# Split-precision mixture-of-experts kernel on one Trainium2 core: first loads and first gate products in another order, down products five steps behind, and f16 parts in one adapter

## What is computed

```python
g = einsum('bsd,edf->ebsf', x, Wg);  u = einsum('bsd,edf->ebsf', x, Wu)
expert_outs = einsum('ebsf,efd->ebsd', silu(g) * u, Wd)
expert_output = einsum('be,ebsd->bsd', gating_probs, expert_outs)
shared = (silu(x @ Sg) * (x @ Su)) @ Sd
x = x + (1 - sg) * expert_output + sg * shared
h = relu(einsum('bsh,bha->bsa', x, W1[lang]) + b1[lang])        # 128 -> 32
y = x + einsum('bsa,bah->bsh', h, W2[lang]) + b2[lang]          # 32 -> 128
x = x + (y - mean(y)) * rsqrt(var(y) + 1e-5) * gamma[lang] + beta[lang]
```

## Time and profile before

| | |
|---|---|
| median of 3 runs | 297.24 us |
| lowest, highest | 296.75, 297.40 us |
| profiled execution, its time | 297.04 us |
| its span, first to last instruction | 295.2 us |
| granted TensorE clock | 0.999 of full speed |
| instructions in the span | 5086 |
| ScalarE busy | 231.1 us, 517 instructions |
| GpSimd busy | 19.3 us, 32 instructions |

### The profile page before, as it was taken

The page is one execution under the profiler, slowest core; times in us unless marked ns, Lnnn a source line. Parts: engine busy times, 40 slices in busy tenths (PEclk is TensorE's granted clock), DMA queues, the critical chain, the costliest instruction groups (busy, mean ns, idle before and its releaser), DMA issues.

```text
span 295.2 us, 5086 instructions
## 1 busy us (share of the span) xinstructions
PE 290.1 (98%) x1510; PEld 144.3 (49%) x1510; DVE 268.8 (91%) x585; ACT 231.1 (78%) x517; POOL 19.3 (7%) x32
## 2 busy tenths in 40 slices
PE   8999999999999999999999999999999999999995
PEld 2444444444444444444444444444444444588883
DVE  5999999998989898988989999999999999977795
ACT  6998878788878787877897788887878876667771
POOL 3200201100000000000002010001100011000011
PEclk9999999999999999999999999999999999999999
DMA  6973110244000000000011001010001110000001
GB/s 208 385 307 109 52 65 19 62 120 112 2 2 0 0 2 0 0 2 1 1 22 26 18 9 39 12 25 19 17 3 39 27 18 10 2 36 3 0 2 36
DMA packets 17940, 13.39 MB, mean 45 GB/s; under 512 B 11486, under 2 KB 15994, under 8 KB 17914
## 3 DMA queue, kind: packets, MB, share of 16 engines
q1 hardware_dynamic: 17482, 12.86, 14.4%
q10 hardware_dynamic: 432, 0.21, 0.2%
HBM read 11.23 MB, written 1.05 MB: 42 GB/s over the span
## 4 chain that ended last, share of the span: by engine, by line
PE 94%; DVE 2%; DMA 1%; SPq 1%; issue 1%; ACT 0%; POOL 0%; POOLq 0%; DVEq 0%
PE moe_ps L449 10%; PE moe_ps L446 10%; PE moe_ps L447 10%; PE gate_ps L400 10%; PE up_ps L426 10%; PE up_ps L431 10%; PE up_ps L423 10%; PE gate_ps L403 10%; PE gate_ps L408 10%; DMA w_full<-weights 1%; DVE hidden L680 1%; PE adapt_ps L458 0%; DVE gx_lo L649 0%; SPq L319 0%; DVE h_lo L686 0%
## 5 line engine op out<-in xcount | busy, mean ns | idle before, releaser
L563 ACT ACTIVATE silu<-gate_ps 128x512 f32<-128x512 f32 (+1 forms) x160 | 88.2, 551 | 45.3 <-PE gate_ps L408 44.3
L680 DVE SCALAR_TENSOR_TENSOR hidden<-silu,up_ps 128x512 f32<-128x512 f32 (+1 forms) x160 | 100.3, 627 | 19.2 <-PE up_ps L431 11.6
L686 DVE TENSOR_TENSOR h_lo<-hidden,h_hi 128x512 f16<-128x512 f32 (+1 forms) x160 | 102.4, 640 | 0.2
L568 ACT ACTIVATE h_hi<-hidden 128x512 f16<-128x512 f32 (+1 forms) x160 | 92.8, 580 | 9.2 <-DVE hidden L680 8.4
L426 PE MATMUL up_ps<-gx_lo,w_hi 128*128 128x512 f16 (+1 forms) x160 | 57.3, 358 | 0.4 <-DVE gx_lo L649 0.4
L400 PE MATMUL gate_ps<-x_hi,w_hi 128*128 128x512 f16 (+1 forms) x160 | 57.4, 359 | 0.0
L431 PE MATMUL up_ps<-gx_hi,w_lo 128*128 128x512 f16 (+1 forms) x160 | 57.3, 358 | 0.0
L423 PE MATMUL up_ps<-gx_hi,w_hi 128*128 128x512 f16 (+1 forms) x160 | 57.3, 358 | 0.0
L403 PE MATMUL gate_ps<-x_lo,w_hi 128*128 128x512 f16 (+1 forms) x160 | 57.3, 358 | 0.0
L446 PE MATMUL moe_ps<-h_hi,w_hi 128*128 128x512 f16 (+1 forms) x160 | 57.3, 358 | 0.0
L449 PE MATMUL moe_ps<-h_lo,w_hi 128*128 128x512 f16 (+1 forms) x160 | 57.3, 358 | 0.0
(11 more groups left out here) (88 smaller groups left out, 148.6 us busy)
## 6 DMA issues: line engine op xcount, KB each, us to landing
w_full<-weights SPq DMA_DIRECT2D x8, 768.0 KB, 9.2
affine_sb<-affine SPq DMA_DIRECT2D x16, 128.0 KB, 2.9
x_full<-xT SPq DMA_DIRECT2D x3, 256.0 KB, 8.6
x<-x_blocks SPq DMA_DIRECT2D x48, 16.0 KB, 1.8
out_dram<-result SPq DMA_DIRECT2D x3, 256.0 KB, 2.1
w_full<-weights SPq DMA_DIRECT2D x4, 128.0 KB, 3.0
w_full<-w2b SPq DMA_DIRECT2D x24, 16.0 KB
w_full<-weights SPq DMA_DIRECT2D x1, 256.0 KB, 3.8
```

The lines of the kernel that those rows point to most:

```text
L563: nc.scalar.activation(silu_slot(n), gate_ps[n % 2][:, 0:STEPS[n][4]], ACT.Silu, scale=1.0 / W_SCALE).then_inc(silu_ready, 1)
L568: nc.scalar.activation(h_slot(h_hi, n), hidden_slot(n), ACT.Copy).then_inc(h_hi_ready, 1)
L680: nc.vector.scalar_tensor_tensor(out=hidden_slot(n), in0=silu_slot(n), scalar=HIDDEN_RESCALE, in1=up_ps[n % 2][:, 0:STEPS[n][4]], op0=ALU. ...
L686: nc.vector.tensor_tensor(h_slot(h_lo, n), hidden_slot(n), h_slot(h_hi, n), ALU.subtract).then_inc(h_lo_ready, 1)
```

## The change

1. **First loads.** SyncE issues both halves of tile 0 first, then weight pieces 1, 2, 3, tile 1, piece 4, and only then the gating probabilities of experts 1 to 7. ScalarE's queue issues piece 0 and then the first gating probabilities.
2. **First gates.** `first_gates` makes gate(0) and gate(1) in halves of 256 columns, six products for the first half of `x` and six for the second.
3. **First splits.** ScalarE does w_hi of piece 1 ahead of the four gx_hi, pieces 2 and 3 after silu of steps 0 and 1, gx_hi of group 1 at steps 1 and 2, and piece 4 at step 3. h_hi and h_lo of step 0 come at step 3, of steps 1 and 2 at step 4, of 3 and 4 at step 5, and from then on one step behind. VectorE does x_lo of the first half ahead of w_lo of piece 0, w_lo of piece 3 at step 0 and of piece 4 at step 3.
4. **Down products.** down(0) to down(7) stand five steps behind, and step 12 has three, down(7), down(8) and down(9). From down(9) on the lag is three as before. `h_hi` and `h_lo` have six slots for four, `hidden` four for three.
5. **Adapter of the last tile's first half.** W1, W2, x2T and h are split into f16 parts, four more operations on ScalarE and four on VectorE: those of W1 at steps 132 and 133, of W2 at 136 and 137, of x2T at 148, of h at 152. TensorE does six products with W1 and four with an f16 identity in place of the two transposes, after step 150, and six with W2, into one bank, after step 154. Relu is at step 151, the copy of x2 at 152, statistics and result each one step later, with one addition for both batches in place of two. W2 lies in `half_w2`. GpSimd sets the row of ones and makes the f16 identity.

The core of the diff:

```diff
+FIRST_LAG = 5
+H_SLOTS = 6
-HIDDEN_SLOTS = 3
+HIDDEN_SLOTS = 4
 def down_at(n):
-    return n + LAG + min(max(n - len(WHOLE) - len(HALVES) // 2, 0), END_LAG - LAG)
+    first = max(FIRST_LAG - LAG - max(n - 2 * CHUNKS + 1, 0), 0)
+    return n + LAG + first + min(max(n - len(WHOLE) - len(HALVES) // 2, 0), END_LAG - LAG)
...
 def in_at(j):
-    return 1 if j < MOVED else 2
+    return 1 if j < MOVED else 3
 def back_at(j):
-    return 6
+    return 6 if j < MOVED else 7
...
+HIDDEN_PARTS_AT = {n + 1: [n] for n in range(5, LAST)}
+HIDDEN_PARTS_AT.update({3: [0], 4: [1, 2], 5: [3, 4]})
...
-            load_first(0)
-            sp.dma_start(cols(x_full, 0, HALF), xT[0, :, 0:HALF]).then_inc(x0_loaded[0], 16)
+            for half in range(2):
+                sp.dma_start(cols(x_full, half, HALF), xT[0, :, half * HALF:(half + 1) * HALF]).then_inc(x0_loaded[half], 16)
             for i in (1, 2, 3):
                 load_first(i)
-                if i == 1:
-                    sp.dma_start(gates_in[:, 2 * B:], gates[:, 2 * B:]).then_inc(gates_loaded, 16)
             sp.dma_start(cols(x_full, 1, N), xT[1]).then_inc(x_loaded[0], 16)
             load_first(4)
+            sp.dma_start(gates_in[:, 2 * B:], gates[:, 2 * B:]).then_inc(gates_loaded, 16)
...
+            def first_gates():
+                pe.wait_ge(w_first_hi_ready, 1)
+                for half in range(2):
+                    x_at = slice(half * HALF, (half + 1) * HALF)
+                    pe.wait_ge(x_hi_ready, half + 1)
+                    for n in range(2):
+                        nc.tensor.matmul(gate_ps[n][:, x_at], expert_w(w_hi, 0, 0, n), x_hi[:, x_at], start=True, stop=False)
...
+            def half_in(j):
+                pe.wait_ge(y_ready, BEFORE[j])
+                pe.wait_ge(half_w1_lo_ready, 1)
+                pe.wait_ge(half_x2T_lo_ready, 1)
+                for of_w, of_x in ((half_w1_hi, half_x2T_hi), (half_w1_lo, half_x2T_hi), (half_w1_hi, half_x2T_lo)):
+                    for q in range(PAIRS):
+                        last = nc.tensor.matmul(fourth(adapt_ps, q)[:, 0:S], cols(of_w, q, A), cols(of_x, q, S),
...
+                for q in range(PAIRS):
+                    nc.tensor.matmul(cols(x2_ps, q, S), cols(half_x2T_hi, q, S), ident_half[:, :], start=True, stop=False)
+                    last = nc.tensor.matmul(cols(x2_ps, q, S), cols(half_x2T_lo, q, S), ident_half[:, :], start=False,
+                                            stop=True)
...
+                    nc.tensor.matmul(psum, h_hi_q, w2_hi_q, start=True, stop=False)
+                    nc.tensor.matmul(psum, h_hi_q, w2_lo_q, start=False, stop=False)
+                    last = nc.tensor.matmul(psum, h_lo_q, w2_hi_q, start=False, stop=True)
...
+            act.dma_start(w_full[:, low:high], weights[0, :, low:high]).then_inc(w0_loaded[0], 16)
+            nc.scalar.preload_act_table(ACT.Silu)
             act.dma_start(gates_in[:, 0:2 * B], gates[:, 0:2 * B]).then_inc(first_gates_loaded, 16)
-            nc.scalar.preload_act_table(ACT.Silu)
-            act.dma_start(cols(x_full, 1, HALF), xT[0, :, HALF:]).then_inc(x0_loaded[1], 16)
```

More of the change, by code:

```diff
@@ L200, in build @@
         x2_ps = bank("x2_ps")
[L201 removed]
+        half_back_ps = moe_ps[(TILES - 1) % 2]
         last_tile = TILES - 1
@@ L460, in adapter_in @@
                 last.then_inc(adapt_done, 1)
-                if j < MOVED:
-                    return
-                pe.wait_ge(consts_ready, 1)
-                for q in range(first, first + count):
-                    last = nc.tensor.transpose(cols(x2_ps, q, S), cols(x2T, q, S), ident[:, :])
-                last.then_inc(x2_transposed, 1)
             def adapter_back(j):
-                _, first, count, _ = JOBS[j]
                 pe.wait_ge(ones_ready, 3)
@@ L478, in adapter_back @@
                     return
-                pe.wait_ge(adapt_h_ready, count)
-                pe.wait_ge(x2_ready, 1)
-                for q in range(first, first + count):
-                    last = nc.tensor.matmul(cols(back_ps[q % 2], q // 2, D), stacked(adapt_h, q, S, A + 1),
-                                            stacked(w2b2_sb, q, D, A + 1), start=True, stop=True)
-                last.then_inc(back_done, 1)
+                half_back()
             pe.wait_ge(warm_ready, 1)
```

194 lines of the change are left out of this document (146 added, 48 removed).

## The result

| | before | changed |
|---|---|---|
| median | 297.62 us (11 runs, 296.75 to 298.54) | 299.3 us (11 runs, 298.77 to 300.54) |
| profiled execution | 297.04 us | 298.9 us |
| its span, granted clock | 295.2 us, 0.999 | 297.0 us, 0.997 |

The changed kernel takes 1.0055 times as long, 95% interval 1.004 to 1.007: slower by 1.64 us. The forecast was slower, 298.3; the time lies above it and just outside the range, which ended at 299.1. 0.38 of the 1.0 us of difference is only the median of before, 297.24 in the three runs shown and 297.62 in these eleven: on the base of 297.24, from which the forecast was added up, the ratio gives 298.9, inside the range. The rest is in the sum, which gave +1.05 where the two spans differ by 1.8.

What follows compares the result with a forecast made beforehand. TensorE was taken as the bound (busy 290.1 of 295.2 us), VectorE close behind. Opening +1.51, adapter -0.46 and end 0 sum to +1.05 on the median 297.24, giving 298.3 us; range 297.1 to 299.1.

Steps and rivals of the forecast that it cites:

- The mechanism: Opening: TensorE reaches step 8 1.29 us of work earlier, stands for VectorE's w_lo of expert 1's up third; chance 0.66.
- the start of gx_hi in the part on the first loads: ScalarE's opening: second weight piece lands at 4.27, w_hi runs from 4.33, gx_hi from about 4.7 instead of 4.31.
- The price of 0.45 for a gx_lo held by GpSimd's x_lo: VectorE's opening: gx_lo at 9.8 held until 10.25 by GpSimd's later x_lo; bounds 0 and 0.9.
- the signs that I had named: Changed trace: step 8 pause, w_lo ending near 20.4, x_lo about 8.9, gx_lo lengthened, L473 of step 4 delayed, adapter 0.55 and 0.33.
- The term: Opening up to step 8: L431 0.22 later with 1.29 still to do, +1.51 us; bounds 0 and +1.9.
- The adapter: Last tile's first half in f16 parts: in -0.16, back -0.19, pause of 0.11 gone; together -0.46, from -0.7 to -0.1.
- the end: Last steps: h_lo(159) ends at about 289.0, where the last product wants it at 289.01; costs 0, at most +0.25.
- the splits of the adapter: Steps 132 to 152: four more operations each on ScalarE and VectorE cost nothing; without cover each up to 0.4.
- the halves: First gates: twelve products of 256 columns, 0.108 each, still start at 4.58 and end at 5.90.
- Rival C: After the step 8 pause: slower clock, 8 products at half pace cost 1.6 more, 299.9; chance 0.05.
- Rivals A: Opening: VectorE closes its gaps, x_lo earlier, gx_lo not held; -0.5 to +0.5 in all, say 297.3; chance 0.23.
- B: Opening: w_lo of expert 1 ends before TensorE wants it, so waits go; -0.98 - 0.46, 295.8; chance 0.06.

Runs made afterwards that it cites:

- lag_three: Changed kernel with down products three steps behind from the start, h_hi and h_lo one behind, expert 0's down piece split at step 1: 298.2 us, 1.0017.
- parts_later: Changed kernel with only h_hi and h_lo of steps 1 to 9 later, one per step to step 8, arrears at steps 9 and 10: 297.99 us, 1.001.
- downs_alone: h_only with the change's down products, hidden parts and slots, and the four gx_hi of group 1 together at step 2: 298.56 us, 1.0038 to before.
- h_only: Kernel before with nothing changed but the f16 adapter of the last tile's first half: 297.1 us, 0.9987.
- downs_repaired: downs_alone with hidden parts four steps behind, caught up at steps 10 to 14, five hidden slots, downs five behind until step 16: 297.3 us, 0.9994.
- gx_first: Changed kernel with ScalarE's four gx_hi of group 0 ahead of w_hi of the second weight piece again: 298.79 us, 1.0041.
- loads_before: Changed kernel with the first loads in the order of the kernel before, ScalarE's and VectorE's orders and the downs as changed: 299.12 us, 1.0051.
- h_only_again: h_only measured once more, in one call with downs_alone and downs_repaired: 297.27 us, 0.9987 of the kernel before.
- later_loads: parts_later with the loads of the kernel before and gx_hi ahead of the second weight piece: 298.36 us, 1.002.

## Why the prediction was right in its sign and 1 us short

**The mechanism was right.** The prediction said that the later down products bring TensorE to step 8 with six products fewer behind it, and that VectorE's w_lo pins it there. lag_three (-1.1 us), parts_later (-1.3), downs_alone (+1.29 on h_only) and downs_repaired (-1.3 on downs_alone) show it four ways, one of them by moving only h_hi and h_lo. With ratios the result can be split: adapter -0.0013, down products' place +0.0051 (downs_alone less h_only), first splits, gates and loads +0.0017 (the changed kernel less downs_alone). In us: -0.4 + 1.5 + 0.5 = 1.6. Taken the other way round, the split is different: first splits, gates and loads +0.0030 (lag_three less h_only), down products' place +0.0038 (the changed kernel less lag_three), 0.9 and 1.1 us. Each of these differences is uncertain by some 0.002. So the down products' place costs 1.1 to 1.5 us, clear of the noise either way; the rest of the opening costs 0.5 to 0.9 beside it, of which only the 0.9 is clear of the noise, and gx_hi's share of that (0.0014, gx_first) is not shown.

**The step that failed is the start of gx_hi in the part on the first loads, above all the landing of the second weight piece.** "Its data is the third issue on SyncE, as before (1.67), and lands 2.6 later at 4.27": it took 3.5, w_hi began at 5.24 instead of 4.33, gx_hi at 5.57 instead of 4.7, L478 of step 0 at 7.61 instead of 6.75. VectorE reached gx_lo of the second group at 10.69 instead of 9.8. Queue place and issue time were as before, and I took the landing time from there too, though the transfers around the piece had changed. For gates_in I had noted that no row has a landing time at its new place; the same held for this piece, whose neighbours had changed. And I left a wait out: gx_hi needs the first coefficients, and the gating probabilities for them had moved behind piece 0 on ScalarE's queue. They were ready at 4.96, so gx_hi could not have begun at 4.7 even with the piece at 4.27; gx_first, where it waits for them alone, has it at 5.01. Of the 0.87 us, 0.3 are thus the coefficients' and 0.56 the piece's. What either costs in the end no run shows by itself: gx_first is not clear of the noise, and in loads_before the piece was late as well.

**A second error took half of it back.** The price of 0.45 for a gx_lo held by GpSimd's x_lo was not there: since VectorE was itself late, gx_lo from 10.69 lay behind x_lo (9.34 to 10.56). The block is real, but it met the w_lo at 8.73 (0.80 for 0.42, beside GpSimd's cast and the start of x_lo). Two of the signs that I had named did not come: no gx_lo was lengthened, and L473 of step 4, at 11.98, waited for nothing. So 0.9 late less 0.45: hidden(3) at 11.74 for 11.35, and from there the offset stays to the end of the chain, 15.79 for 15.34, 20.18 for 19.72, L478 at 20.93 for 20.43. Carrying VectorE's queue on at 0.60 and 0.26 was therefore right within 0.1 us over 8.5 us. The term came to +2.01, not +1.51, just above its own upper end of +1.9. (The forecast's own range was also added up wrong: +0.9 and -0.7 on 297.24 give a low end of 297.4, not 297.6.)

**The adapter** came to -0.24 for -0.46, inside its range; with the 0.05 at 164 us the stretch came to -0.28. In: -0.11 for -0.16; the two batches' products do run side by side (six products from 279.32 to 279.60, 0.28 for 0.33), but the entry still costs 0.09. Back: +0.01 for -0.19. Its six products take 0.058 each, for 0.055 in the sum; what I left out is 0.10 ahead of the first and 0.08 behind the last. The 0.33 was a sum of products, the 0.52 a stretch with its edges, and the two can't be subtracted. For the same term the Trainium skill (FP8 and Floating Point Precision, TensorE Precision Notes) counts four passes for a true f32 product, and the estimate worked out from that gave 0.15 less gain, -0.31: nearer to the -0.24 measured than my -0.46, though for the part back not even that little was gained, and no run here separates passes from edges.

So of the 0.75 us between the sum and the two spans, 0.50 is the opening, 0.18 the stretch with the adapter, and 0.07 lies behind the last down product, where the sum had nothing.

**Right as predicted:** the end (h_lo ends at 290.59 and the last product, at 290.74, doesn't wait), the splits of the adapter cost nothing on ScalarE and VectorE, GpSimd's late coefficients (x_lo at 9.34, predicted 8.9), the halves. Rival C fell: the granted clock is 1.00 after the pause of step 8 and products follow at 0.215; h_only_again even had a pause of 1.25 before its L482 at 11.57, and its next product came 0.23 later. Rivals A and B needed a VectorE that comes earlier; it came later. That the splits of the adapter cost nothing is read from TensorE, which up to the last down product loses nothing but at the adapter's own edges.

**Open:** whether later_loads is slower than parts_later at all, which has a worse order of loads on paper (1.002 and 1.001, whose intervals overlap). In the two profiles its step 8 ends 0.3 later, and its two w_lo beside GpSimd take 1.04 us longer together. And why the second weight piece lands later in some kernels: the order of the loads goes with it (last section), but the one pair that differs in it alone, the changed kernel and loads_before, has 3.5 and 3.3.

## What to carry over

Before giving an engine other work earlier, look up what it will want next and whether its supplier can deliver by then: here down products were moved out of the way of short waits, less than 1 us in all, and the engine then arrived 1.29 us of work earlier at a w_lo that came no earlier. Here, with both engines busy for over 90%, the order in the second one's queue decided; the repair was to put what is wanted next ahead of what is only due (parts_later, one table, -1.3 us), not to free the first. Look up, too, everything that a moved operation waits for, not only the wait that was moved on purpose: gx_hi had two. And a landing time taken from a row holds for the traffic of that row: with other neighbours it needs a range, here 2.6 to 3.9 us.
